# Attention's end and the routed feed-forward's start: scatters split, one normalisation moved to VectorE, unread matmuls, weights loaded later

## Chip, cores and metric

The kernel runs on one NeuronCore of one Trainium2 chip. The metric is the device time of one execution in microseconds (us); of several executions the median is taken.

## The reference, cut to what matters

The input x has two batches of 1024 rows of 256 values. Four pairs of layers follow one another, each `x = x + attention(layernorm(x))` and then `x = x + feed_forward(layernorm(x))`, with a context of 77 rows per batch. The change touches the last pair.

```
scores = einsum(Q, K) * scale + rel_pos_bias      # 16 heads, 77 keys
attn = softmax(where(mask, scores, -1e9))
x = x + (attn @ V, all heads) @ Wo
xf = layernorm(x)
eid = argmax(softmax(xf @ router_w + router_b))   # one of 8 experts
rank = number of earlier rows with the same expert
valid = rank < 320
y_e = relu(buf_e @ w1_e + b1_e) @ w2_e + b2_e     # rows that are valid
yov = relu(xf @ ow1 + ob1) @ ow2 + ob2            # rows over an expert's 320
x = x + where(valid, y_e, yov)
```

`ow1` and `ow2` are the overflow weights: they serve the rows that found their expert full.

## The kernel before, in words

x lives in SBUF as 16 tiles of 128 rows (`c.x`); the tiles of batch 0 are worked on first (`TOKEN_ORDER`), 8 of them (`HALF`), then those of batch 1. Each engine (SP for DMAs, POOL, DVE, ACT, PE) has its own program, and a step of one waits for semaphores that another raises.

**The last attention** (`attn_gqa`, L2046 to L2468) is a software pipeline over t = 0 to 15. In step t PE makes the scores of tile t (L2382). DVE adds the bias out of PSUM (L2195, L2197), takes the row maxima (L2200) and subtracts them (L2201); ACT takes the exponential (L2300); DVE sums it per head (L2211) and inverts the sums (L2212). POOL multiplies the probabilities by these inverses: that is the normalisation (L2108), 128x1232 values in place. Then PE transposes the probabilities (`prob_transpose`, L2396) in three groups, ACT copies them out of PSUM (L2307 to L2310), and PE multiplies them with the folded value weights (`output`, L2405, 10 products of two records each). DVE adds the result to x (L2206) and takes its statistics (L2265). POOL also adds the two halves of the rotary embedding of the next tile (L2105) ahead of each normalisation. The order on POOL's queue is that of its program: in step 14 (`t == NT - 2`) these are the rotary addition of tile 15, the normalisation of tile 14, and then the eight scatters of batch 0. In PE's program, the step after the last tile (`t == NT`, L2451) begins with 18 products whose results nobody reads (`keep_warm`, L107 to L110, bf16, 512 columns each), followed by the transposes of tile 15.

**Routing of batch 0** is woven into the same steps: router logits, expert and slot of each row are found while batch 1 is still in attention. `scatter_tile` (L1111, L1114) then writes one tile of 128 rows to its slots in the DRAM table `expert_rows`, by an indirect DMA out of POOL's queue, and raises `c.scat`. The slots come from L1083 (`r_slot_ok`).

**The last stage** (`moe3`, L2473 to L2840) is a block of its own, after the attention's block has ended on all engines and its semaphores are cleared (`free_semaphores`, L171 to L175). Its front: DVE finds the statistics (L200 to L215) and normalises the 8 tiles of batch 1 (L2609); PE transposes them (L2748) with ACT copying (L2712); PE makes the router logits (L1092, `pe_logits`) and turns them back (L1100); DVE finds experts and slots in a chain of some 25 small operations; POOL scatters the eight tiles of batch 1 (L1114). Meanwhile SP has loaded the small vectors, w1 and w2 of experts 0 and 1, and `ow1` (2 DMAs, L2545) and `ow2` (L2546). Then SP waits for all 16 scatters (`sp.wait_ge(c.scat, 16 * NT)`, L2547) and loads the rows of experts 0 to 3 and the overflow rows (L2534, L2540, L2553).

The body: for each of 8 experts DVE normalises the rows (L2640), PE transposes them (`x_transpose`, L2765), DVE copies (L2648 to L2651), PE makes the hidden layer (`hidden`, L2775, 32 records) with ACT's relu (L2722), and then the outputs (L2788, L2797), which DVE finishes and POOL writes to the output (L2580). w1 of expert e+2 is loaded by SP once `hidden(e)` is done (L2557, L2526). The overflow rows come last, in a loop (L2818 to L2840) that first waits for `ow_in` (L2816).

Of the kernel before, what the change touches and what calls it, by code (L numbers as in the profile page):

```python
# [6 lines left out]
P = 128  # L7
ALU = mybir.AluOpType
# [11 lines left out]
NT = T // P  # L20
# [5 lines left out]
HALF = NT // 2  # L26
PAD = 4
KC = D // P
SK = 77
# [25 lines left out]
def inside(i):  # L55

    return not is_static(i) or 0 <= i < NT
# [1988 lines left out]
def attn_gqa(c, d):  # L2046
# [48 lines left out]
    @programs.gpsimd  # L2095
    def _(pool):
        ng = nc.gpsimd

        def step(t, q):
            b = q % 2  # L2100
            if inside(t + 1) and t + 1 >= 1:
                i = t + 1
                pool.wait_ge(s["roped"], i + 1)
                wait(pool, s["qT_ps"], i * 2)
                ng.tensor_tensor(qr[:, :], t1[:, :], t2[:, :], ALU.add).then_inc(s["rope_ok"], 1)  # L2105
            if inside(t):
                pool.wait_ge(s["rd_ok"], t + 1)
                ng.tensor_tensor(heads(c.prob[b]), heads(c.prob[b]),  # L2108
                                 rden[b][:, :].unsqueeze(2).to_broadcast([P, HB, SK]), ALU.mult).then_inc(s["p_ok"], 1)
            if t == NT - 2:  # L2110
                pool.wait_ge(s["r_slot_ok"], 1)
                for k in range(HALF):
                    scatter_tile(c, r, k)
        for t in range(-1, NT):
            step(t, t % 4)

    @programs.vector
    def _(dve):
# [89 lines left out]
        def sums(t, b):  # L2208
            dve.wait_ge(s["exp_ok"], t + 1)
            wait(dve, s["p_ok"], t - 1)  # L2210
            links(nv.reduce_sum(c.den[:, :], heads(c.prob[b]), AX))  # L2211
            nv.reciprocal(rden[b][:, :], c.den[:, :]).then_inc(s["rd_ok"], 1)  # L2212

        layer_norm(1, 1)
        batch0 = slice(0, HALF)
# [129 lines left out]
    def _(pe):  # L2345
# [97 lines left out]
        def step(t, q):  # L2443
            b = q % 2
            banks_read(t)
            if inside(t):
                scores(t, b)
            if inside(t - 1):
                if t - 1 in (0, HALF):
                    pe.wait_ge(vw_in[t // HALF], 16 * 2)  # L2450
                if t == NT:  # L2451
                    keep_warm(c, c.ps[3], 18)
                prob_transpose(t - 1, 1 - b)
            if inside(t + 2):
                lnT(t + 2, b)
            if inside(t - 1):
                output(t - 1, 1 - b)
            if inside(t + 1):
                q_transpose(t + 1, 1 - b)
            route(t)  # L2460
            if inside(t + 2):
                queries(t + 2, b)
            back(t)
        step(-2, 2)
        keep_warm(c, c.ps[0], 12)
        for t in range(-1, NT + 1):
            step(t, t % 4)
    return programs  # L2468


# [2 lines left out]
def moe3(c, d):  # L2473
# [41 lines left out]
    with nc.Block() as block:  # L2515
        @block.sync
        def _(sp):
# [23 lines left out]
            for e in range(2):  # L2541
                load_w1(e)
                load_w2(e)
            for k in range(KC):
                sp.dma_start(ow1[:, k, :], d["L3_ffn_ow1"][k * P:(k + 1) * P, :]).then_inc(s["ow_in"], 16)  # L2545
            sp.dma_start(ow2[:, :, :], d["L3_ffn_ow2"].rearrange("(m p) n -> p m n", p=P)).then_inc(s["ow_in"], 16)  # L2546
            sp.wait_ge(c.scat, 16 * NT)  # L2547
            load_x(0)
            load_third(0)
            for e in range(1, 4):  # L2550
                load_x(e)
            load_third(1)
            sp.dma_start(Xo[:, :].rearrange("p (r n) -> p r n", n=XW),  # L2553
                         xd[OV0:OV0 + OVX * P, :].rearrange("(r p) n -> p r n", p=P)).then_inc(s["ox_in"], 16)
            for e in range(E3):
                if e + 2 < E3:
                    sp.wait_ge(s["h_ps"], e * MH + MH)  # L2557
                    load_w1(e + 2)
                if e % 2 == 1 and e + 2 < E3:
                    sp.wait_ge(s["y_ps"], third(e // 2) + 1)  # L2560
                    load_w2(e + 1)
                    load_w2(e + 2)
                if e >= 1 and e + 3 < E3:
                    for r in range(2):
                        written(sp, chunk(e - 1, r))
                    load_x(e + 3)
                if e % 2 == 0 and e >= 2 and e // 2 + 1 < E3 // 2:
                    written(sp, third(e // 2 - 1))
                    load_third(e // 2 + 1)
# [171 lines left out]
        def _(pe):  # L2741
            nt = nc.tensor

            def ln_transpose(n, k):
                pe.wait_ge(s["ln_ok"], n + 1)
                wait(pe, s["lnT_ok"], n - 2)
                for h in range(KC):
                    last = nt.transpose(c.ps[T3[n % 3]][:, h * P:(h + 1) * P], c.lnk[:, k * D + h * P:k * D + (h + 1) * P],  # L2748
                                        c.ident[:, :])
                last.then_inc(s["lnT_ps"], 1)  # L2750
            for n, k in enumerate(range(HALF, NT)):
                ln_transpose(n, k)
            pe.wait_ge(s["lnT_ok"], HALF)
# [47 lines left out]
            def over_transpose(n):  # L2801
                pe.wait_ge(s["oxl_ok"], n + 1)
                for k in range(KC):
                    last = nt.transpose(c.ps[0][:, k * P:(k + 1) * P], XLo[:, k * P:(k + 1) * P], c.ident[:, :])
                last.then_inc(s["oT_ps"], 1)
            x_transpose(0)
            for e in range(E3):
                hidden(e)
# [193 lines left out]
```

## Time and profile before

| what | value |
|---|---|
| median of 3 runs | 1050.93 us (1049.06 to 1051.18) |
| the profiled execution's own time | 1051.14 us |
| its span in the trace | 1049.3 us |
| PE busy | 910.5 us, 87% of the span |
| DVE busy | 714.4 us, 68% |
| POOL busy | 382.8 us, 36% |
| ACT busy | 377.4 us, 36% |
| mean granted TensorE clock | 0.95 of full |

The span is what the trace covers; the execution's own time is 1.84 us longer. A part by part account is made in the trace's time and then set against 1051.14. "PEclk" is the share of full TensorE clock that the chip granted: 1.00 is 2.4 GHz, 0.50 is 1.2 GHz, and a value between says that the clock changed inside the stretch. The page's line of 40 slices (26.2 us each) reads

```profile
PEclk9899989999989997988999999999999758999999
```

The two lowest digits, 7 and 5, stand in slices 32 and 33, from 813 to 866 us: the end of attention and the front of the last stage.

### The profile page before, as it was taken

Reading aid. Unit: us, or ns where it says so; the run is one execution under the profiler, and the core shown is the slowest. Engines: PE = TensorE matmul, PEld = TensorE weight load, DVE = VectorE, ACT = ScalarE, POOL = GpSimd, SP = SyncE. Lnnn points to the kernel's source line nnn. Section 1 sums busy time; section 2 is a strip of 40 time slices with the busy share of each in tenths; the row PEclk is TensorE's granted clock in tenths of the full one; section 3 lists DMA queues with packets and bytes.
Section 4 is the critical chain, followed back from the end, with each engine's and each line's share of the span. In section 5 each row is a group of like instructions: output and inputs, shape, how many; then the busy total and the mean of one; then the engine's idle time right before and its main releaser. Section 6 shows DMA issues by size and latency. Waiting matters only on the chain. (4 is left out here: it accounts for less than half of the span.)

```text
span 1049.3 us, 17056 instructions
## 1 busy us (share of the span) xinstructions
PE 910.5 (87%) x5799; PEld 648.5 (62%) x5803; DVE 714.4 (68%) x1579; ACT 377.4 (36%) x851; POOL 382.8 (36%) x282
## 2 busy tenths in 40 slices
PE   3899879999889985868899889999998619999997
PEld 2677744444567763743588467777766407777787
DVE  6788858888778877888377799999988222221211
ACT  2466541000155555753455143434333202213122
POOL 1566503423546642517355223333334220111111
PEclk9899989999989997988999999999999758999999
DMA  5000069999400007203465651111110294425300
GB/s 174 1 1 0 1 205 303 324 322 315 160 1 1 0 1 184 80 11 108 125 199 168 212 159 49 49 49 49 49 31 29 74 320 147 157 94 176 106 13 19
DMA packets 87256, 117.14 MB, mean 112 GB/s; under 512 B 12464, under 2 KB 75949, under 8 KB 86781
## 3 DMA queue, kind: packets, MB, share of 16 engines
q1 hardware_dynamic: 77455, 88.15, 27.7%
q10 hardware_dynamic: 4408, 15.46, 4.3%
q0 software_dynamic: 5328, 12.70, 3.4%
q8 instruction: 37, 0.61, 0.2%
q14 instruction: 28, 0.23, 0.1%
HBM read 68.08 MB, written 50.16 MB: 113 GB/s over the span
## 5 line engine op out<-in xcount | busy, mean ns | idle before, releaser
L925 PE MATMUL psum<-m_W,lnT 128*128 128x512 f32 x256 | 114.2, 598 | 0.8 <-DVE acc L837 0.8
L405 POOL TENSOR_TENSOR prob<-prob,a_rden 128x1232 f32<-128x1232 f32 x32 | 71.9, 2248 | 80.3 <-DVE a_rden L477 80.3
L925 PEld LDWEIGHTS psum<-m_W,lnT 128*128 128x128 f32 x256 | 47.2, 190 | 59.1 <-issue 56.7
L2722 ACT ACTIVATE prob<-psum,x_b 128x320 f32<-128x320 f32 x64 | 33.7, 527 | 127.5 <-PE psum L2775 127.5
L2405 PE MATMUL psum<-g_VW,pT 128*128 128x256 f32 (+1 forms) x320 | 75.3, 391 | 1.6 <-ACT pT L2310 1.6
L2775 PE MATMUL psum<-x_xT,x_w 128*128 128x320 f32 x256 | 72.7, 443 | 1.3 <-DVE x_xT L2649 1.3
L910 POOL TENSOR_TENSOR m_masked<-m_rel,m_mrow 128x1232 f32<-128x1232 f32 x16 | 41.8, 2616 | 79.8 <-DMA masked_bias<-m_masked 62.5
L2580 POOL DMA_INDIRECT out_x<-x_yt,x_X x20 | 19.8, 992 | 138.2 <-DVE x_yt L2663 138.2
L2405 PEld LDWEIGHTS psum<-g_VW,pT 128*128 128x128 f32 (+1 forms) x320 | 60.9, 194 | 13.3 <-ACT pT L2310 5.3
L2108 POOL TENSOR_TENSOR prob<-prob,g_rden 128x1232 f32<-128x1232 f32 x16 | 36.0, 2249 | 77.1 <-DVE g_rden L2212 77.1
L2775 PEld LDWEIGHTS psum<-x_xT,x_w 128*128 128x128 f32 x256 | 49.5, 195 | 23.0 <-issue 4.4
L2105 POOL TENSOR_TENSOR g_qr<-g_t 128x1024 f32<-128x1024 f32 x15 | 35.4, 2360 | 76.5 <-DVE g_t L2179 76.5
L2360 PE MATMUL psum<-g_Wq,lnT 128*128 128x512 f32 x128 | 59.6, 609 | 0.5 <-ACT lnT L2290 0.5
L2788 PE MATMUL psum<-x_w,prob 128*128 128x256 f32 x256 | 56.6, 379 | 0.0
L456 DVE TENSOR_REDUCE mx<-psum 128x16 f32<-128x1232 f32 x32 | 45.6, 1425 | 15.3 <-PE psum L595 15.1
L1275 POOL DMA_INDIRECT routed_results<-pT,m_idx x39 | 38.4, 984 | 38.8 <-issue 21.7
L2788 PEld LDWEIGHTS psum<-x_w,prob 128*128 128x128 f32 x256 | 48.0, 190 | 6.2
L396 POOL TENSOR_SCALAR ln<-x_tiles,mean,rstd 128x256 f32<-128x256 f32 x32 | 41.6, 1299 | 27.5 <-DVE rstd L426 25.6
L462 DVE TENSOR_TENSOR prob<-psum,mx 128x616 f32<-128x616 f32 x64 | 48.2, 794 | 3.0
L474 DVE TENSOR_REDUCE den<-prob 128x16 f32<-128x1232 f32 x32 | 45.7, 1427 | 4.4 <-ACT prob L517 4.1
L523 ACT ACTIVATE pT<-psum 128x512 f32<-128x512 f32 (+1 forms) x96 | 43.6, 527 | 13.7 <-PE psum L610 13.7
L2660 DVE TENSOR_TENSOR x_yt<-psum,x_b 128x256 f32<-128x256 f32 (+1 forms) x24 | 10.2, 424 | 52.3 <-PE psum L2788 41.3
(441 smaller groups left out, 2083.2 us busy)
## 6 DMA issues: line engine op xcount, KB each, us to landing
routed_rows<-hole SPq DMA_DIRECT2D x8, 2210.0 KB, 34.8
masked_bias<-m_masked ACTq DMA_DIRECT2D x16, 616.0 KB, 7.5
g_bias<-masked_bias SPq DMA_DIRECT2D x16, 616.0 KB, 3.8
x_w<-in_L_ffn_w SPq DMA_DIRECT2D x16, 512.0 KB, 4.6
x_w<-in_L_ffn_w SPq DMA_DIRECT2D x8, 1024.0 KB, 7.7
m_xb<-routed_rows SPq DMA_DIRECT2D x39, 130.0 KB, 2.1
m_rel<-in_rel_bias ACTq DMA_DIRECT2D x8, 616.0 KB, 9.8
expert_rows<-hole SPq DMA_DIRECT2D x1, 4680.0 KB, 35.3
```

The costliest lines, as they stand in the source:

```text
L396: nc.gpsimd.tensor_scalar(c.ln[b][:, :], xt(c, i), mean_of(c, i), rstd_of(c, i), ALU.subtract, ALU.mult).then_inc(ln_ok, 1)
L405: nc.gpsimd.tensor_tensor(heads(c.prob[b]), heads(c.prob[b]), rden[b][:, :].unsqueeze(2).to_broadcast([P, H, SK]), ALU.mult).then_inc(norm ...
L456: nv.reduce_max(c.mx[:, :].rearrange("p (r h) -> p r h", r=GROUPS), sview.rearrange("p r (h k) -> p r h k", k=SK), AX).then_inc(mx_ok, 1)
L462: nv.tensor_tensor(c.prob[b].rearrange("p (r h k) -> p r h k", r=GROUPS, k=SK)[:, r], sview[:, r].rearrange("p r (h k) -> p r h k", k=SK), ...
L474: nv.reduce_sum(c.den[:, :], heads(c.prob[b]), AX).then_inc(den_ok, 1)
L523: na.activation(c.pT[b][:, j0 * P:j1 * P], bank_pT[g][:, 0:(j1 - j0) * P], ACT.Copy).then_inc(pT_ok, 1)
L910: nc.gpsimd.tensor_tensor(masked[i % 2][:, :, :], rel[i // 2 % 2][:, :, :], mrow[:, i % 2, :].unsqueeze(1).to_broadcast([P, HB, SK]), ALU. ...
L925: last = nt.matmul(c.ps[p][:, :], c.lnT[b][:, k * P:(k + 1) * P], W[:, k, p * 512:(p + 1) * 512], start=(k == 0), stop=(k == KC - 1))
L2360: last = nt.matmul(c.ps[3 + u][:, :], c.lnT[b][:, k * P:(k + 1) * P], Wq[:, k, u * 512:(u + 1) * 512], start=(k == 0), stop=(k == KC - 1))
L2405: last = nt.matmul(bank_y[:, 0:D], c.pT[b][0:w, j * P:(j + 1) * P], VW[0:w, i // HALF, j, :], start=(j == 0), stop=(j == NB - 1))
L2775: last = nt.matmul(c.ps[2 + m % 4][:, 0:CAP], w1[b][:, k, m * P:(m + 1) * P], xT[b][:, k, :], start=(k == 0), stop=(k == KC - 1))
L2788: last = nt.matmul(c.ps[6 + ch % 2][:, 0:D], hT[b][:, m, r * P:(r + 1) * P], w2[b][:, m, :], start=(m == 0), stop=(m == MH - 1))
```

## The change

Six edits, all between the last two tiles of attention and the first expert:

1. POOL's step 14 issues the scatters of tiles 0 to 2 ahead of the normalisation of tile 14, and those of tiles 3 to 7 behind it.
2. The normalisation of tile 15 is done by DVE, right behind the inversion of its sums. POOL normalises tiles 0 to 14.
3. The 18 unread products ahead of the last `prob_transpose` become 8, and 6 are added behind the last `output`.
4. PE's program in the last stage begins with 10 unread products.
5. Behind the overflow transposes' definition, ahead of `x_transpose(0)`, PE waits for all 16 scatters and then issues 12 unread products.
6. SP loads `ow1` and `ow2` behind the rows of experts 0 to 3 and the overflow rows, instead of ahead of the wait for the scatters.

```diff
@@ attn_gqa, POOL @@
-            if inside(t):
+            if t == NT - 2:
+                pool.wait_ge(s["r_slot_ok"], 1)
+                for k in range(3):
+                    scatter_tile(c, r, k)
+            if inside(t) and t < NT - 1:
                 pool.wait_ge(s["rd_ok"], t + 1)
                 ng.tensor_tensor(heads(c.prob[b]), heads(c.prob[b]),
                                  rden[b][:, :].unsqueeze(2).to_broadcast([P, HB, SK]), ALU.mult).then_inc(s["p_ok"], 1)
             if t == NT - 2:
-                pool.wait_ge(s["r_slot_ok"], 1)
-                for k in range(HALF):
+                for k in range(3, HALF):
                     scatter_tile(c, r, k)
@@ attn_gqa, DVE, sums @@
             nv.reciprocal(rden[b][:, :], c.den[:, :]).then_inc(s["rd_ok"], 1)
+            if t == NT - 1:
+                dve.wait_ge(s["rd_ok"], t + 1)
+                nv.tensor_tensor(heads(c.prob[b]), heads(c.prob[b]), rden[b][:, :].unsqueeze(2).to_broadcast([P, HB, SK]),
+                                 ALU.mult).then_inc(s["p_ok"], 1)
@@ attn_gqa, PE @@
                 if t == NT:
-                    keep_warm(c, c.ps[3], 18)
+                    keep_warm(c, c.ps[3], 8)
                 prob_transpose(t - 1, 1 - b)
...
         for t in range(-1, NT + 1):
             step(t, t % 4)
+        keep_warm(c, c.ps[3], 6)
@@ moe3, SP @@
-            for k in range(KC):
-                sp.dma_start(ow1[:, k, :], d["L3_ffn_ow1"][k * P:(k + 1) * P, :]).then_inc(s["ow_in"], 16)
-            sp.dma_start(ow2[:, :, :], d["L3_ffn_ow2"].rearrange("(m p) n -> p m n", p=P)).then_inc(s["ow_in"], 16)
             sp.wait_ge(c.scat, 16 * NT)
...
                          xd[OV0:OV0 + OVX * P, :].rearrange("(r p) n -> p r n", p=P)).then_inc(s["ox_in"], 16)
+            for k in range(KC):
+                sp.dma_start(ow1[:, k, :], d["L3_ffn_ow1"][k * P:(k + 1) * P, :]).then_inc(s["ow_in"], 16)
+            sp.dma_start(ow2[:, :, :], d["L3_ffn_ow2"].rearrange("(m p) n -> p m n", p=P)).then_inc(s["ow_in"], 16)
@@ moe3, PE @@
+            keep_warm(c, c.ps[3], 10)
             for n, k in enumerate(range(HALF, NT)):
                 ln_transpose(n, k)
...
+            pe.wait_ge(c.scat, 16 * NT)
+            keep_warm(c, c.ps[3], 12)
             x_transpose(0)
```

## Rows read from the trace of the kernel before

**Rows 1.** Windows of 2 us: busy us (xcount) by engine, PEclk, DMA share, GB/s

```profile
820.00:822.00 2.00, 0.19 (x1) 0.19 (x2) 0.00 (x0) 0.00 (x0) 1.75 (x1) 0.97 0.19 67
...
834.00:836.00 2.00, 0.00 (x0) 0.00 (x0) 1.51 (x9) 1.37 (x2) 0.00 (x0) 0.88 0.11 19
...
872.00:874.00 2.00, 2.00 (x7) 1.31 (x6) 0.00 (x0) 0.53 (x1) 0.00 (x0) 0.73 0.68 221
```

**Rows 2.** The timeline, last but one tile of attention (start us, us, engine, line, what)

```profile
798.89 2.36 POOL L2105 TENSOR_TENSOR g_qr<-g_t 128x1024 f32<-128x1024 f32 x1 [5.47 <-DVE g_t L2179]
...
801.73 1.44 DVE L2201 TENSOR_TENSOR prob<-prob,mx 128x1232 f32<-128x1232 f32 x1
...
806.27 2.25 POOL L2108 TENSOR_TENSOR prob<-prob,g_rden 128x1232 f32<-128x1232 f32 x1 [5.02 <-DVE g_rden L2212]
...
808.58 1.09 PE L2396 MATMUL psum<-ident,prob 128*128 128x128 f32 x8 [0.75 <-POOL prob L2108]
...
810.87 1.44 DVE L2201 TENSOR_TENSOR prob<-prob,mx 128x1232 f32<-128x1232 f32 x1
...
810.95 4.59 PE L2405 MATMUL psum<-g_VW,pT 128*128 128x256 f32 x20 [0.53 <-ACT pT L2310]
...
811.26 1.89 POOL L1114 DMA_INDIRECT expert_rows<-x_tiles,acc  x1 [0.30 <-issue]
...
814.72 0.96 POOL L1114 DMA_INDIRECT expert_rows<-x_tiles,acc  x1 [0.30 <-issue]
...
815.08 0.25 DVE L2212 RECIPROCAL g_rden<-den 128x16 f32<-128x16 f32 x1
```

**Rows 3.** The timeline, last tile of attention and the end of that block

```profile
815.59 3.83 PE L110 MATMUL psum<-RQ,identb 128*128 128x512 bf16 x17
...
819.50 2.25 POOL L2108 TENSOR_TENSOR prob<-prob,g_rden 128x1232 f32<-128x1232 f32 x1
...
821.81 2.52 PE L2396 MATMUL psum<-ident,prob 128*128 128x128 f32 x10 [2.39 <-POOL prob L2108]
...
824.86 6.47 PE L2405 MATMUL psum<-g_VW,pT 128*128 128x256 f32 x20 [0.53 <-ACT pT L2310]
...
831.89 0.41 DVE L2265 BATCH_NORM_STATS2 bst<-x_tiles 128x6 f32<-128x256 f32 x1
```

**Rows 4.** The timeline, start of the last stage and its first TensorE work

```profile
833.87 1.28 ACT L220 ACT_TABLE_LOAD   x1 [9.06 <-PEq L175]
...
836.27 3.67 PE L2748 MATMUL psum<-ident,lnk 128*128 128x128 f32 x16 [4.95 <-DVE lnk L2609]
...
840.42 1.93 PE L1092 MATMUL psum<-lnT_all,qT 128*32 128x256 f32 x16 [0.47 <-ACT lnT_all L2712]
```

**Rows 5.** The timeline, the same logits products for batch 0, earlier

```profile
774.49 1.07 PE L1092 MATMUL psum<-lnT_all,qT 128*32 128x256 f32 x16
```

**Rows 6.** The timeline, from the first load of routed rows to expert 0

```profile
860.81 0.38 SPq L2534 DMA_DIRECT2D x_X<-expert_rows  x1
...
865.89 1.54 PE L2765 MATMUL psum<-ident,x_XL 128*128 128x128 f32 x6 [20.53 <-DVE x_XL L2640]
...
868.76 10.98 PE L2775 MATMUL psum<-x_xT,x_w 128*128 128x320 f32 x32 [1.33 <-DVE x_xT L2649]
```

**Rows 7.** Loads of routed rows between 859 and 868 us (tile view)

```profile
DMA to landing us min/median/max: 2.6/3.2/4.2
```

**Rows 8.** The timeline, the same two steps of expert 1 and 2, later

```profile
886.93 8.78 PE L2775 MATMUL psum<-x_xT,x_w 128*128 128x320 f32 x32
...
895.54 0.82 PE L2765 MATMUL psum<-ident,x_XL 128*128 128x128 f32 x6
```

**Rows 9.** The timeline of SP's queue, and TensorE at expert 2

```profile
842.07 4.80 SPq L2545 DMA_DIRECT2D x_ow<-in_L_ffn_ow  x2
...
879.78 16.77 SPq L2526 DMA_DIRECT2D x_w<-in_L_ffn_w  x4
...
906.80 8.88 PE L2775 MATMUL psum<-x_xT,x_w 128*128 128x320 f32 x32
```

## Prediction

> **What bounds the kernel now.** I read the page's clock line first, then the windows, then the timeline between 795 and 907 us. TensorE is busy nearly everywhere, so time can only be won where it waits or runs at half clock. All six edits lie in the one stretch where it does both.
>
> In the last attention, each tile goes from the inverse sums through the normalisation to the transposes and the output. For tile 14 this is tight: normalisation at 806.27, transposes at 808.58, output ending at 810.95 + 4.59 = 815.54, all at full clock [rows 2]. For tile 15 the inverse is ready at 815.33 [rows 2], but POOL starts its normalisation at 819.50, since eight scatters stand ahead of it; the transposes begin at 821.81, after a pause of 2.39 us [rows 3]. The clock fell from 2.4 to 1.2 GHz inside 820 to 822, after TensorE had done 0.19 us of work in those 2 us [rows 1]. Transposes and output then took 821.81 to 824.86 + 6.47 = 831.33, that is 9.52 us, where tile 14 took 815.54 - 808.58 = 6.96.
>
> The last stage begins at 833.87 [rows 4], 1.57 us after DVE's last work of the old block (832.30) [rows 3]. The clock fell again between 834 and 836, with no TensorE work there [rows 1], so the first transposes and the logits products ran at half clock [rows 4]; the same products took 1.07 us for batch 0 [rows 5] and 1.93 here. After that come DVE's chain and POOL's eight scatters, which no edit touches. Then rows are loaded from 860.81, and the first `x_transpose` and most of `hidden(0)` run at half clock until inside 872 to 874 [rows 1, 6].
>
> **Part by part.**
>
> Edits 1 and 2, the normalisations. The new start of tile 15's transposes is the later of two. DVE: the inverse ends at 815.33; the multiplication has the shape and the two SBUF inputs of L2201, 1.44 us [rows 2], so it is done at 816.82. TensorE: its unread products start at 815.59, 18 of them in 3.83 us (17 are recorded), 0.213 each [rows 3]; 8 take 1.70, until 817.30. The later one is 817.30. The gain is 821.81 - 817.30 = **4.51**. What is late next is thus TensorE itself, with 0.48 us in hand against DVE. Queued behind DVE's multiplication is the residual of tile 14, some 1.5 us later than now; output 15 waits for it, but only 2.37 us after its transposes start, so it is hidden by 2 us.
>
> POOL's queue: the rotary addition ends at 801.25, the slots come from step 13, so three scatters go from about 801.4 on, and the normalisation of tile 14 is wanted at 806.27 [rows 2]. A scatter costs 0.96 and 0.30 between two [rows 2], so three end near 805.2. One scatter of eight took 1.89: it was issued at 811.26, inside an L2201 that ran from 810.87 to 812.31 [rows 2], and ended 0.84 after it. The second of the three falls inside the L2201 at 801.73; stretched likewise it ends at 804.0 and the third at 805.3. Normalisation 14 keeps its start: cost **0**. Bounds: a gain is excluded, since 806.27 is set by DVE's inverse; if all three took 1.89 with 0.30 between, the third would end at 801.4 + 6.3 = 807.7, costing 1.4. I take 0, the bound next to the one collision the trace shows.
>
> Whether the first scatter, under way when L2201 starts, would hold up DVE no row shows well. The Trainium skill (SBUF — State Buffer, "SBUF: two separate sides") says that a DVE instruction with two SBUF inputs and a GpSimd instruction that reads SBUF lock each other out, whichever started first holding the shared ports to its end. The stretched scatter agrees with that.
>
> Edit 3, clock. With no pause ahead of tile 15, transposes and output should take tile 14's 6.96 us instead of 9.52: gain **2.56** (bounds 0 and 2.56), end at 824.26. The 6 products behind the output take 1.28, to 825.54; DVE's tail of 832.30 - 831.33 = 0.97 would end at 825.23. The block now ends with TensorE, 0.31 later: cost **0.31** (0 if the barrier hides it).
>
> Edit 4. Ten products at full clock take 2.13 us, from 833.87 to 836.00 in old time, and the first transposes start at 836.27 when DVE has a tile ready [rows 4]: hidden, by 0.27. Only 1.6 us without TensorE work now lie before them, instead of 831.33 to 836.27, so I expect full clock. Logits: 1.93 - 1.07 = **0.86** [rows 4, 5]. Transposes: 16 in 3.67, two a tile, 0.46; ACT copies tile by tile behind them and will set the pace, so I count half of one tile, **0.25** (bounds 0 and 1.8, half of 3.67).
>
> Edit 5. The wait asks for what the row loads wait for anyway, and only `x_transpose(0)` is queued behind it. Twelve products start at about 860.81; all at half clock they take 12 x 0.426 = 5.11, until 865.92, against transposes at 865.89 [rows 6]: cost 0.03 at most, and nothing once the clock rises. At full clock the six transposes take 0.82 instead of 1.54, gain **0.72**, and `hidden` 8.78 to 8.88 instead of 10.98, gain **2.15** [rows 6, 8, 9]. The rise in the kernel before came after some 4.3 us of steady products (868.76 to about 873) [rows 1, 6], and the twelve last about that long. Bounds: 0 and 2.87.
>
> Edit 6. SP's three issues move behind the row loads; the two of `ow1` took 4.80 us of SP's time [rows 9]. The next that SP has to do is w1 of expert 2 at 879.78, used at 906.80: 27 us in hand [rows 9]. The overflow step is 140 us away. In their old place they kept the DMA queues busy until shortly before the row loads. These landed in 2.6 to 4.2 us [rows 7]; at best all come at 2.6, a gain of up to 1.6. I take **0**.
>
> Sum: 4.51 + 2.56 - 0.31 + 0.86 + 0.25 + 0.72 + 2.15 = **10.74** gained. The profiled execution's own time is 1051.14, which gives 1040.4; that execution lies 0.21 above the median of 1050.93, inside the spread of the runs. About 0.2% (2.1 us) is what a measurement of this kernel can tell from no change.
>
> **Rivals.**
>
> A. The warm-up ahead of the experts misses: the clock rises late, or falls again in the 1.3 us in which DVE copies between transposes and `hidden(0)`. For it: twelve products last barely as long as the rise took before. The 2.87 is lost: 1043.3. Chance 0.12.
>
> B. The clock is at half when the last stage starts. The ten products take 4.26, until 838.13, the transposes start 1.86 late, and 0.86 + 0.25 is lost: 1043.4. Against it: the six products in front are meant to bridge, and the pause is shorter than the 2.39 us before the fall at 820 to 822. Chance 0.08.
>
> C. Tile 15 still runs at half clock: 2.56 lost, 1043.0. Against it: no pause of over 1 us is left there. Chance 0.05.
>
> D. The first scatter holds DVE's ports: L2201 at 801.73 waits until the scatter ends near 802.4, 0.7 us, and the inverse, normalisation 14 and all behind it move along: 1041.1. For it: two SBUF inputs against a descriptor write. Against it: the scatter before the stretched one was still running when the L2201 of 810.87 started, and that one kept its 1.44 [rows 2]. By the Trainium skill's section just named, the first to start holds the ports for its whole instruction; the trace shows no DVE instruction held up. Chance 0.08.
>
> E. Slower. The late overflow weights push w1 of expert 2 out. The place is SP's queue and the DMA queues between the overflow rows and L2526, and it decides once w1 lands after 906.80 in old time: the 27 us must be used up first. To end slower by 2.1 it would have to use them up and add 13 more, as with 15 more: 1055.4. Nothing in the trace lasts like that; SP's longest two issues are 4.80. Chance 0.02.
>
> F. The edits do not do what they say: tile 15 starts early, but a wait further on, such as the block's end or the row loads, takes the gain back, within 2.1 of before: 1050. The timeline shows no second chain that long. Chance 0.02.
>
> **The numbers.** My forecast, 1040.4, has 0.63, and by the small bounds lies between 1038.8 (row loads 1.6 shorter) and 1041.8 (normalisation 14 late by 1.4). The range 1038.8 to 1043.5 takes in A, B, C and D; two of the clock rivals together would leave it. All of these are faster: 0.96. Same is F, 0.02; slower is E, 0.02.
>
> **What would show it.** Right: three scatters between 801 and 806; normalisation 14 at 806.3; transposes of tile 15 at 817.3 with a granted clock of 1.00 to the end of output; the last stage 6.8 us earlier, its logits products near 1.07 us; `x_transpose(0)` 7.9 us earlier than 865.89, at 0.82 us; `hidden(0)` near 8.8 us; nothing changed behind it. Wrong: a clock of 0.50 in any of these, a pause of TensorE at expert 2, a DVE step 14 that is late, or a gain in a stretch that I left alone.

## The result and the profile after

The changed kernel took 1041.24 us in the median of 5 runs (1039.85 to 1043.00), the kernel before 1049.06 in the median of 5 on the same chip (1047.06 to 1051.18). The ratio is 0.9926, 95% interval 0.9904 to 0.9948: faster by 0.5 to 1.0%. The profiled execution took 1039.85 us, 11.3 less than the profiled one of before; the medians differ by 7.8. Why these two differ is taken up below. The ratios in this document leave out executions that lie more than 1.5% above the fastest of the same kernel.

The page's first line, and its clock line in slices of 26 us, after the change:

```profile
span 1038.1 us, 17090 instructions
...
PEclk9899989999989997987999999999999969999999
```

The dip of 7 and 5 in slices 32 and 33 has become 9 and 6. The timeline of the same execution (start us, us, engine, line, what), from step 14 of attention to expert 0:

```profile
800.96 1.01 POOL L1114 DMA_INDIRECT expert_rows<-x_tiles,acc  x1 [0.15 <-issue]
...
801.28 1.44 DVE L2204 TENSOR_TENSOR prob<-prob,mx 128x1232 f32<-128x1232 f32 x1
...
802.27 1.29 POOL L1114 DMA_INDIRECT expert_rows<-x_tiles,acc  x1 [0.30 <-issue]
...
803.87 0.96 POOL L1114 DMA_INDIRECT expert_rows<-x_tiles,acc  x1 [0.30 <-issue]
...
805.01 3.29 PE L2389 MATMUL psum<-g_KB,g_qT 128*128 128x154 f32 x16 [2.50 <-ACT g_qT L2303]
...
805.83 2.24 POOL L2112 TENSOR_TENSOR prob<-prob,g_rden 128x1232 f32<-128x1232 f32 x1 [1.01 <-DVE g_rden L2215]
...
808.13 2.31 PE L2403 MATMUL psum<-ident,prob 128*128 128x128 f32 x10
...
812.07 1.55 POOL L1114 DMA_INDIRECT expert_rows<-x_tiles,acc  x1 [0.30 <-issue]
...
815.55 0.25 DVE L2215 RECIPROCAL g_rden<-den 128x16 f32<-128x16 f32 x1
...
815.62 1.67 PE L110 MATMUL psum<-RQ,identb 128*128 128x512 bf16 x7
...
815.84 1.44 DVE L2218 TENSOR_TENSOR prob<-prob,g_rden 128x1232 f32<-128x1232 f32 x1
...
817.34 1.09 PE L2403 MATMUL psum<-ident,prob 128*128 128x128 f32 x8
...
819.71 4.59 PE L2412 MATMUL psum<-g_VW,pT 128*128 128x256 f32 x20 [0.53 <-ACT pT L2317]
...
827.14 1.28 ACT L220 ACT_TABLE_LOAD   x1 [7.49 <-PEq L175]
...
829.55 2.71 PE L2756 MATMUL psum<-ident,lnk 128*128 128x128 f32 x16
...
832.74 1.07 PE L1092 MATMUL psum<-lnT_all,qT 128*32 128x256 f32 x16 [0.47 <-ACT lnT_all L2720]
...
849.78 0.96 POOL L1114 DMA_INDIRECT expert_rows<-x_tiles,acc  x1 [0.30 <-issue]
...
852.24 0.38 SPq L2542 DMA_DIRECT2D x_X<-expert_rows  x1
...
852.27 4.45 PE L110 MATMUL psum<-RQ,identb 128*128 128x512 bf16 x10 [15.45 <-DMA expert_rows<-x_tiles,acc]
...
857.36 0.88 PE L2774 MATMUL psum<-ident,x_XL 128*128 128x128 f32 x6
...
859.58 8.85 PE L2784 MATMUL psum<-x_xT,x_w 128*128 128x320 f32 x32 [1.33 <-DVE x_xT L2657]
```

Three scatters now lie ahead of the normalisation of tile 14, which starts at 805.83 (before: 806.27 [rows 2]). Tile 15 is normalised by DVE at 815.84, its transposes start at 817.34 (before: 821.81 [rows 3]), and its output takes 4.59 instead of 6.47. The last stage starts at 827.14 (before: 833.87 [rows 4]), its first transposes take 2.71 instead of 3.67, its logits products 1.07 instead of 1.93, and the hidden layer of expert 0 takes 8.85 instead of 10.98 [rows 4, 6].

The windows of 2 us (busy us and instructions of PE, PEld, DVE, ACT, POOL; PEclk; DMA share; GB/s):

```profile
806.00:808.00 2.00, 2.00 (x11) 1.92 (x9) 0.51 (x3) 0.00 (x0) 2.00 (x1) 0.57 0.00 0
...
822.00:824.00 2.00, 2.00 (x11) 1.77 (x10) 0.00 (x0) 0.00 (x0) 0.00 (x0) 1.00 0.00 0
...
858.00:860.00 2.00, 0.67 (x5) 0.38 (x4) 1.72 (x6) 0.00 (x0) 0.00 (x0) 1.00 0.93 286
```

The clock is full through tile 15's output and through the copies ahead of the hidden layer. It was at half for a while between 806 and 810, where the profiled execution of before was at full. That slowed tile 15's scores, which PE makes in this stretch, and tile 14's transposes (2.31 us for all ten, where before they ran from 808.58 to 810.42, 1.84 us). The scores of before:

```profile
805.46 2.36 PE L2382 MATMUL psum<-g_KB,g_qT 128*128 128x154 f32 x16 [2.48 <-ACT g_qT L2296]
```

In the thirteen other profiles of this document, the kernels that keep POOL's old order among them, the same scores took 3.22 to 4.03 us. So the change didn't bring this half clock: the one execution without it is the one that the prediction read.

To compare executions, I cut each into the same pieces, from starts and ends in the timeline. Each piece ends where the next begins: A, start of tile 14's normalisation to tile 15's transposes; B, to the end of tile 15's output; C, to the start of the last stage; D, to the end of its logits products; E, to the first load of rows; F, to DVE's first work on them; G, to the hidden layer of expert 0; H, to the transposes of expert 1. "Rest" is all behind that, "start" the time at which A begins.

| kernel (profiled execution) | start | A | B | C | D | E | F | G | H | A to H | rest |
|---|---|---|---|---|---|---|---|---|---|---|---|
| before | 806.27 | 15.54 | 9.52 | 2.54 | 8.48 | 18.46 | 3.96 | 3.99 | 10.83 | 73.32 | 169.71 |
| change | 805.83 | 11.51 | 6.96 | 2.84 | 6.67 | 18.43 | 3.93 | 3.41 | 8.69 | 62.44 | 169.83 |
| change, again | 804.95 | 11.98 | 6.96 | 2.84 | 6.67 | 18.49 | 4.04 | 3.33 | 10.38 | 64.69 | 169.76 |
| change, third | 810.68 | 11.49 | 6.95 | 2.85 | 6.67 | 18.44 | 3.64 | 3.72 | 8.68 | 62.44 | 169.78 |
| moves alone | 810.40 | 13.57 | 6.89 | 2.55 | 8.27 | 18.42 | 4.03 | 4.00 | 10.63 | 68.36 | 169.74 |
| unread alone | 808.73 | 14.68 | 9.99 | 2.85 | 6.66 | 19.85 | 3.83 | 3.32 | 8.69 | 69.87 | 169.80 |
| late weights alone | 805.61 | 15.20 | 8.59 | 2.54 | 8.43 | 18.47 | 4.21 | 3.99 | 10.60 | 72.03 | 169.76 |
| change, weights early | 806.00 | 12.11 | 6.96 | 2.84 | 6.66 | 19.77 | 3.87 | 3.32 | 8.69 | 64.22 | 169.78 |
| change, no twelve | 807.36 | 11.80 | 6.96 | 2.85 | 6.66 | 18.77 | 3.96 | 4.00 | 10.26 | 65.26 | 169.78 |
| change, no six and ten | 807.53 | 11.44 | 6.96 | 2.53 | 7.77 | 18.45 | 3.87 | 3.33 | 8.69 | 63.04 | 169.83 |
| change, POOL normalises | 810.09 | 13.12 | 6.96 | 2.85 | 6.67 | 18.47 | 3.42 | 3.33 | 8.69 | 63.51 | 169.80 |
| products throughout | 809.57 | 11.97 | 6.95 | 2.85 | 6.66 | 18.45 | 4.96 | 3.33 | 8.69 | 63.86 | 169.77 |
| the same, again | 809.86 | 11.55 | 6.95 | 2.85 | 6.67 | 18.46 | 4.45 | 3.32 | 8.69 | 62.94 | 169.80 |
| change, four between | 812.24 | 11.88 | 6.96 | 2.85 | 6.66 | 18.44 | 3.72 | 3.32 | 8.69 | 62.52 | 169.84 |

Two things stand out. The rest is 169.7 to 169.8 in all fourteen: nothing behind expert 0's hidden layer changed. And the start of A lies anywhere between 805.0 and 812.2, with no order by kernel. Of the edits only the three scatters lie ahead of it, and they don't set it: it follows the start of DVE's inverse by 0.33 or 0.34 us in all fourteen. The chip may have a part in it, since the four executions on one chip start at 805.0 to 810.4 and the three on another at 809.9 to 812.2.

The ratios below can't rank the changed kernel and its variants: all their intervals overlap. What an edit is worth is therefore read from the pieces, of one execution per variant.

### The profile page after: what moved, and what is told of

Its sections match the earlier page's. It is cut to its first block and busy times, and to the rows that moved or that the text cites. A ratio compares the mean times of both kernels' runs of the same rounds, so it can differ in the third digit from the quotient of the medians.

```text
span 1038.1 us, 17090 instructions
## 1 busy us (share of the span) xinstructions
PE 912.5 (88%) x5815; PEld 648.8 (63%) x5821; DVE 713.1 (69%) x1580; ACT 377.0 (36%) x851; POOL 382.1 (37%) x281
## 5 line engine op out<-in xcount | busy, mean ns | idle before, releaser
L2784 PE MATMUL psum<-x_xT,x_w 128*128 128x320 f32 x256 | 70.6, 434 | 1.3 <-DVE x_xT L2657 1.3
L2112 POOL TENSOR_TENSOR prob<-prob,g_rden 128x1232 f32<-128x1232 f32 x15 | 33.7, 2249 | 73.1 <-DVE g_rden L2215 73.1
L840 DVE SCALAR_TENSOR_TENSOR acc<-psum,gates,acc 128x256 f32<-128x256 f32 x96 | 40.3, 477 | 9.6 <-PE psum L925 9.5
```

What stands on the lines that cost most here:

```text
L2784: last = nt.matmul(c.ps[2 + m % 4][:, 0:CAP], w1[b][:, k, m * P:(m + 1) * P], xT[b][:, k, :], start=(k == 0), stop=(k == KC - 1))
```

## The experiments

**The change again, twice.** No edit. First:

> The changed kernel once more, beside the kernel before on the same chip. The two profiled executions differed by 11.3 us, the medians of five runs by 7.8. Theory: the profiled execution of before was one with more half clock than most (the clock falls at slightly different moments in each execution), so the typical gain is the 7 to 9 us of the medians. Rival: the medians were off by drift between chips, and the gain is the 10.7 us of the prediction. Theory: ratio near 0.9920; rival: near 0.9898.

Measured: ratio 0.9938 (0.9912 to 0.9964), over 34 runs of before that lay between 1044.54 and 1056.22. The interval holds the theory's 0.9920 and leaves out the rival's 0.9898. But the theory's reason covers only a part: the profile shows that the changed kernel, too, can lose time inside the stretch. TensorE's timeline of that execution:

```profile
857.05 0.88 PE L2774 MATMUL psum<-ident,x_XL 128*128 128x128 f32 x6 [0.31 <-DVE x_XL L2648]
...
859.26 10.54 PE L2784 MATMUL psum<-x_xT,x_w 128*128 128x320 f32 x32 [1.33 <-DVE x_xT L2657]
```

and its windows (columns as above):

```profile
856.00:858.00 2.00, 1.61 (x9) 0.74 (x7) 1.03 (x4) 0.00 (x0) 0.00 (x0) 0.97 0.95 303
858.00:860.00 2.00, 0.74 (x2) 0.63 (x3) 1.76 (x6) 0.00 (x0) 0.00 (x0) 0.88 0.88 276
860.00:862.00 2.00, 2.00 (x5) 1.22 (x5) 0.00 (x0) 0.43 (x1) 0.00 (x0) 0.50 1.07 370
```

The six transposes ran at full clock, and then the clock fell inside 858 to 860, in the pause of 1.33 us in which DVE copies. The hidden layer took 10.54 us. This is rival A of the prediction. Of the seven profiled executions that have the twelve products and nothing between transposes and hidden layer, it is the only one (H of 10.38; 8.68 or 8.69 in the other six).

The third:

> The changed kernel a third time. Theory: its stretch from tile 14's normalisation to the end of expert 0's hidden layer is 62.4 us where the clock holds into the hidden layer and 64.7 where it falls, and all the rest of the spread between executions (several us) arises ahead of that normalisation, which started between 805.0 and 810.4 us in the profiles so far. Rival: the stretch itself varies by over 3 us.

Measured: ratio 0.9894 (0.9861 to 0.9927). Its stretch A to H is 62.44, the same as the first one's, though A starts 4.85 later. The stretches of the three executions differ by 2.25 at most, so the rival's 3 us was not seen. Of the 2.25, 1.69 lie in H, by the clock ahead of expert 0, as the theory said; 0.47 more lie in A, which the theory left out. The interval of the ratio holds both the 0.9920 and the 0.9898 of the first expectation, so the question of the typical gain is open again; it is taken up below. One small cost shows here: the rows landed early (F of 3.64), the twelve products were still running, and G is 3.72 instead of 3.3 to 3.4.

**The moves alone** (edits 1 and 2 on the kernel before):

```diff
+            if t == NT - 2:
+                pool.wait_ge(s["r_slot_ok"], 1)
+                for k in range(3):
+                    scatter_tile(c, r, k)
-            if inside(t):
+            if inside(t) and t < NT - 1:
...
+            if t == NT - 1:
+                dve.wait_ge(s["rd_ok"], t + 1)
+                nv.tensor_tensor(heads(c.prob[b]), heads(c.prob[b]), rden[b][:, :].unsqueeze(2).to_broadcast([P, HB, SK]),
+                                 ALU.mult).then_inc(s["p_ok"], 1)
```

> The kernel before with the two moves of edits 1 and 2 alone (three scatters ahead of normalisation 14, tile 15 normalised by DVE); unread products and weight loads as before. Theory of the prediction: the transposes of tile 15 now start where the 18 unread products end, 3.83 us behind 815.6, so 2.4 us are won, and with the pause gone its 2.56 us of half clock: 4.9 us in all, ratio 0.9953. Rival, the clock alone matters and the moves win nothing by themselves: ratio 1.000. Second rival, the moves carry the whole change: ratio 0.992 or lower.

Measured: ratio 0.9971 (0.9952 to 0.9991), stretch 68.36, that is 4.96 less than before. TensorE's timeline:

```profile
826.28 4.58 PE L2412 MATMUL psum<-g_VW,pT 128*128 128x256 f32 x20 [0.53 <-ACT pT L2317]
...
835.82 3.67 PE L2755 MATMUL psum<-ident,lnk 128*128 128x128 f32 x16 [4.95 <-DVE lnk L2616]
```

The output is back at 4.58 us with no new product at all: once the pause is gone the clock holds. The front is untouched, 3.67 as before. The ratio's interval holds the theory's 0.9953 at the edge and excludes both rivals. That the stretch came so close to 4.9 is partly luck: A gave 1.97 where the theory had 2.4, B gave 2.63 where it had 2.56, and 0.41 came from D and H, which these edits don't touch.

**The unread products alone** (edits 3, 4 and 5 on the kernel before):

```diff
-                    keep_warm(c, c.ps[3], 18)
+                    keep_warm(c, c.ps[3], 8)
...
+        keep_warm(c, c.ps[3], 6)
...
+            keep_warm(c, c.ps[3], 10)
...
+            pe.wait_ge(c.scat, 16 * NT)
+            keep_warm(c, c.ps[3], 12)
```

> The kernel before with edits 3, 4 and 5 alone (unread products 8 instead of 18, and 6, 10 and 12 new ones). Theory: the front gains 1.1 us and expert 0 up to 2.9 us of full clock, less 0.3 for the block's end; tile 15 still waits for POOL: 3.7 us, ratio 0.9965. Rival: with only 8 products ahead of a pause of 4.5 us the clock falls earlier there and the gain is 2 us or less, ratio 0.998 or above.

Measured: ratio 0.9974 (0.9950 to 0.9997), stretch 69.87, 3.45 less than before. The interval holds both expectations; the pieces tell more. D and H came down as the theory said (6.66 and 8.69), B went up a little (9.99), as the rival said, and E went up by 1.4, which nobody had said. A is 0.86 shorter for no reason of these edits: POOL's eight scatters took 9.95 us in this execution and 10.80 in that of before, where one was stretched to 1.89. The timeline, with tile 15's output, the last scatter and the first load behind it:

```profile
825.83 7.57 PE L2405 MATMUL psum<-g_VW,pT 128*128 128x256 f32 x20 [0.53 <-ACT pT L2310]
...
858.93 0.96 POOL L1114 DMA_INDIRECT expert_rows<-x_tiles,acc  x1 [0.30 <-issue]
...
862.76 0.38 SPq L2535 DMA_DIRECT2D x_X<-expert_rows  x1
```

and the windows there:

```profile
858.00:860.00 2.00, 0.00 (x0) 0.00 (x0) 0.00 (x0) 0.00 (x0) 1.59 (x2) 0.50 1.07 398
...
860.00:862.00 2.00, 0.00 (x0) 0.00 (x0) 0.00 (x0) 0.00 (x0) 0.00 (x0) 0.50 0.90 341
```

The last scatter needs 3.83 us from its issue to the load that waits for it, where the changed kernel needs 852.24 - 849.78 = 2.46, and the DMA share is still 0.90 in 860 to 862. (In the changed kernel it was 0.18 to 0.37 between 846 and 852.)

**The late weights alone** (edit 6 on the kernel before: the three loads of `ow1` and `ow2` behind that of the overflow rows).

> The kernel before with edit 6 alone (overflow weights loaded behind the row loads). Theory: nothing, ratio 1.000 within 0.001. Rival: with the DMA queues free the row loads land up to 1.6 us earlier, ratio 0.9985.

Measured: ratio 1.000 (0.9979 to 1.0021). E and F are 18.47 and 4.21, against 18.46 and 3.96: no load came earlier. The theory holds. What its stretch has less than before (1.29) lies in A and B, ahead of the edit, in pieces at half clock. Since this edit does nothing there, its profile is a second sample of the kernel before: 73.3 and 72.0.

**The change with the weights early** (edit 6 alone undone), run because of the 19.85 above:

```diff
+            for k in range(KC):
+                sp.dma_start(ow1[:, k, :], d["L3_ffn_ow1"][k * P:(k + 1) * P, :]).then_inc(s["ow_in"], 16)
+            sp.dma_start(ow2[:, :, :], d["L3_ffn_ow2"].rearrange("(m p) n -> p m n", p=P)).then_inc(s["ow_in"], 16)
             sp.wait_ge(c.scat, 16 * NT)
```

> The changed kernel with edit 6 undone: the overflow weights loaded ahead of the wait for the scatters again. In the run with the unread products alone, which has the weights early, the time from the end of the logits products to the first load of rows was 19.85 us, against 18.4 to 18.8 in all other profiles, because the last scatter landed 3.83 us after its issue instead of 2.4. Theory: the faster front moves the last scatter into the time in which the overflow weights still fill the DMA queues, so edit 6 is worth 1.4 us with edits 3 and 4 and nothing without them: here 19.8 us, and the stretch 63.8 instead of 62.4. Rival: that was chance, here 18.5 and 62.4.

Measured: E is 19.77; ratio to the kernel before 0.9932 (0.9909 to 0.9955). Last scatter and first load:

```profile
850.53 0.96 POOL L1114 DMA_INDIRECT expert_rows<-x_tiles,acc  x1 [0.30 <-issue]
...
854.34 0.38 SPq L2542 DMA_DIRECT2D x_X<-expert_rows  x1
```

3.81 us between them, as with the unread products alone. The stretch is 64.22, of which 0.6 is a longer half clock in A (12.11 against 11.51); without it 63.6. The theory stands, twice seen: edit 6 is worth 1.3 to 1.4 us, but only together with the faster front. In the kernel before, the last scatter was issued 858.37 - 833.87 = 24.5 us after the stage's start and was complete 2.44 us later, at 860.81; in these two kernels it was issued 22.6 to 22.7 us after the start. The times from issue to landing of the stage's eight scatters (tile view of `expert_rows`, POOL alone) show the cause more directly:

| kernel | shortest | median | longest |
|---|---|---|---|
| before | 2.4 | 5.1 | 5.9 |
| change, weights early | 3.8 | 5.5 | 6.0 |
| change | 2.4 | 2.7 | 4.9 |

With the overflow weights in flight at least half of the scatters take over 5 us, in the kernel before too. There the last of the weight loads, issued at 846.91, landed 11.9 us later, at 858.8, 0.4 us behind the issue of the last scatter, which then needed only 2.4; and the last one to land decides when the row loads start. Here that load was issued at 841.01 and landed 12.5 us later, at 853.5, 3 us behind the issue of the last scatter.

**The change without the twelve** (edit 5 undone):

```diff
-            pe.wait_ge(c.scat, 16 * NT)
-            keep_warm(c, c.ps[3], 12)
             x_transpose(0)
```

> The changed kernel without edit 5 (no wait and no 12 unread products ahead of the first transposes of the experts). From the start of tile 14's normalisation to the end of expert 0's hidden layer the profiled changed kernel took 62.4 us in one execution and 64.7 in another, in which the clock fell again ahead of the hidden layer. Theory: without the twelve, transposes and most of the hidden layer run at half clock always: 65.3 us. Rival: the twelve win nothing on average, because the clock rises and falls anyway: under 64 us here too.

Measured: ratio to before 0.9939 (0.9910 to 0.9968), stretch 65.26, the theory's 65.3. TensorE:

```profile
859.48 1.54 PE L2774 MATMUL psum<-ident,x_XL 128*128 128x128 f32 x6 [20.77 <-DVE x_XL L2648]
...
862.36 10.42 PE L2784 MATMUL psum<-x_xT,x_w 128*128 128x320 f32 x32 [1.34 <-DVE x_xT L2657]
```

Against 0.88 and 8.85 in the changed kernel. The agreement of the sum is partly luck (A and E are 0.3 longer here than in the changed kernel, for no reason of this edit). The other three executions without the twelve (before, moves alone, late weights alone) are like this one: G of 3.99 or 4.00, H of 10.60 to 10.83. By G and H together, 14.26 here and 14.59 to 14.82 in those three, the twelve win 1.9 to 2.8 us where the clock holds (12.01 to 12.40) and 0.55 to 1.1 where it falls (13.71).

**The change without the six and the ten** (the second half of edit 3 and edit 4 undone):

```diff
-        keep_warm(c, c.ps[3], 6)
...
-            keep_warm(c, c.ps[3], 10)
```

> The changed kernel without the 6 unread products behind the last output and without the 10 at the start of the last stage. Theory: the block ends 0.3 us earlier, and the front (start of the last stage to the end of its logits products, 6.7 us in the changed kernel) is back at half clock and takes 8.5. Rival: the pause is now short enough by itself, since tile 15 ends at full clock, and the front stays at 6.7 to 7.2.

Measured: ratio to before 0.9917 (0.9888 to 0.9945). C is 2.53 instead of 2.84, the 0.3 as expected. D is 7.77, between the 8.5 of the theory and the 7.2 of the rival:

```profile
830.88 3.67 PE L2755 MATMUL psum<-ident,lnk 128*128 128x128 f32 x16 [4.95 <-DVE lnk L2616]
...
835.02 1.21 PE L1092 MATMUL psum<-lnT_all,qT 128*32 128x256 f32 x16 [0.47 <-ACT lnT_all L2719]
```

The transposes ran at half clock as in the kernel before (3.67), and the clock rose just ahead of the logits products (1.21). The sixteen products thus win 1.10 in D and give back 0.31 in C: 0.8 us in this execution, up to 1.5 where the clock rises later, as in the kernel before. What the six and the ten win each by themselves was not tried.

**The change with POOL normalising tile 15** (edit 2 undone, the scatters split):

```diff
-            if inside(t) and t < NT - 1:
+            if inside(t):
...
-            if t == NT - 1:
-                dve.wait_ge(s["rd_ok"], t + 1)
-                nv.tensor_tensor(heads(c.prob[b]), heads(c.prob[b]), rden[b][:, :].unsqueeze(2).to_broadcast([P, HB, SK]),
-                                 ALU.mult).then_inc(s["p_ok"], 1)
```

> The changed kernel with tile 15 normalised by POOL again, its scatters still split. Theory: POOL's last scatter ends 0.9 us before the inverse is ready, so the normalisation starts 5 ns to 0.1 us behind it and takes 2.25 instead of 1.44: the transposes of tile 15 start 0.8 us later, nothing else changes. Rival: moving the work to DVE is what wins the 4.5 us, and without it the transposes start 3 us later or more.

Measured: ratio to before 0.9914 (0.9882 to 0.9947), stretch 63.51. Inverse, normalisation and transposes:

```profile
820.57 0.25 DVE L2215 RECIPROCAL g_rden<-den 128x16 f32<-128x16 f32 x1
...
820.91 2.24 POOL L2112 TENSOR_TENSOR prob<-prob,g_rden 128x1232 f32<-128x1232 f32 x1 [2.27 <-DVE g_rden L2215]
...
823.21 0.86 PEld L2399 LDWEIGHTS psum<-ident,prob 128*128 128x128 f32 x8 [1.94 <-POOL prob L2112]
```

From the start of the inverse to the transposes it is 2.64 us, in the changed kernel 817.34 - 815.55 = 1.79: 0.85 more, as the theory had it, and far from the rival's 3 us. The split of the scatters is what wins; the move to DVE adds 0.85 to it. (The other 0.76 by which A is longer here lies ahead of the inverse: tile 15's scores took 4.00 us, against 3.29.)

**Products through the whole pause.** Since the clock can fall ahead of expert 0, TensorE was kept at unread products from the moment the slots are known:

```diff
+            pe.wait_ge(s["slot_ok"], 1)
+            keep_warm(c, c.ps[3], 40)
             pe.wait_ge(c.scat, 16 * NT)
-            keep_warm(c, c.ps[3], 12)
+            keep_warm(c, c.ps[3], 18)
             x_transpose(0)
+            keep_warm(c, c.ps[3], 4)
```

> The changed kernel with unread products through the whole pause ahead of the experts: 40 once the slots are known, 18 instead of 12 once all scatters have landed, and 4 between the first transposes and the first hidden layer. Theory: the clock is full by the time the rows arrive and stays so, in every execution; the hidden layer takes 8.8 us, the stretch from tile 14's normalisation to its end 62.3 us, and the median is 1 us below the changed kernel's. Rival: the clock falls at the copies all the same, or the products delay the transposes by over 0.5 us, and nothing is won.

> The kernel with unread products through the whole pause, again, beside the changed kernel on one chip. In its first profile the clock held, but the first routed rows arrived 4.96 us after the issue of their load, against 3.4 to 4.2 in all other profiles. Theory: chance; this time 4.2 or less, the stretch at 62.5 us, and a median 1 us below the changed kernel's. Rival: the many products delay the loads (their instructions have to be fetched too): again 4.7 or more, and no gain over the changed kernel.

Measured: ratios to before 0.9901 (0.9861 to 0.9940) and 0.9916 (0.9884 to 0.9948); the changed kernel beside the second had 0.9894 (0.9861 to 0.9927). The clock held both times, H is 8.69. But the first rows came late both times, 4.96 and 4.45 us after the issue of their load:

```profile
844.79 10.29 PE L110 MATMUL psum<-RQ,identb 128*128 128x512 bf16 x40 [3.89 <-DVE acc L1083]
...
856.34 0.38 SPq L2542 DMA_DIRECT2D x_X<-expert_rows  x1
...
860.79 1.06 DVE L2648 TENSOR_SCALAR x_XL<-x_X 128x256 f32<-128x256 f32 x3 [14.82 <-DMA x_X<-expert_rows]
```

The second theory asked for 4.2 or less and its rival for 4.7 or more; 4.45 is neither. In the other twelve profiles the piece is 3.4 to 4.2, so these two lie above all of them. The traces bear out the rival's reason in part. In the 1 us from 857.34 of the second (and likewise from 857.45 of the first) the DMA view has one packet of 0.02 MB on the queue that it calls "instruction" (q8), and no other profile has one from 8 us ahead of the first row load to 9 us behind it. In both, one of SP's issues of row loads took longer than usual: 1.32 and 0.91 us, against 0.59 at most in the changed kernel. So it looks as if the products cost what they bring, but that this packet, and not something else, held up the load is not shown. No gain over the changed kernel was measured.

**Four products between** the first transposes and the hidden layer, the twelve kept:

```diff
             x_transpose(0)
+            keep_warm(c, c.ps[3], 4)
```

> The changed kernel with 4 unread products between the first transposes and the first hidden layer, the 12 ahead of them kept. Theory: the pause of 1.3 us in which the clock fell in one execution is filled with 0.9 us of work, so the hidden layer takes 8.8 to 9.3 us in every execution, and the stretch 62.4 us. Rival: the clock has not always risen by then, and the hidden layer still takes over 9.5 us in some.

Measured: ratio to before 0.9917 (0.9888 to 0.9946), stretch 62.52, the hidden layer at full clock:

```profile
863.86 0.87 PE L2774 MATMUL psum<-ident,x_XL 128*128 128x128 f32 x6
...
864.57 1.03 PE L110 MATMUL psum<-RQ,identb 128*128 128x512 bf16 x4
...
866.07 8.85 PE L2784 MATMUL psum<-x_xT,x_w 128*128 128x320 f32 x32 [0.47 <-DVE x_xT L2657]
```

The pause shrinks from 1.33 to 0.47 us at no cost (H and G as in the best executions). But this is one profile, and without the four the clock held in six of seven. That the four prevent the fall is not shown; the timing, with a spread of several microseconds between executions, can't tell 0.7 us.

## Why the prediction was right, and where not

The predicted 1040.4 lies 0.8 from the median, and the range held it. That it lies so near is partly luck: the forecast started from 1051.14, 2.1 above the median of before measured beside the change (1049.06), and took off 10.7, where the medians differ by 7.8. Term by term, in the profiled pair:

| term | predicted | measured |
|---|---|---|
| earlier transposes of tile 15 | 4.51 | 4.03 |
| tile 15 at full clock | 2.56 | 2.56 |
| block ends with TensorE | -0.31 | -0.30 |
| logits products, transposes of the front | 0.86 + 0.25 | 1.81 |
| transposes and hidden layer of expert 0 | 0.72 + 2.15 | 2.72 |
| late weights | 0 | 0.06 |
| sum | 10.74 | 10.88 |

The start of A came 0.44 earlier and the rest took 0.12 longer, which makes the 11.2 of the spans. The sums agree better than their terms, since what the first term has too much the fourth has too little.

**Edits 1 and 2.** The mechanism was as told: with POOL's scatters out of the way, tile 15's transposes start when DVE and TensorE are done. One step of it was wrong: "What is late next is thus TensorE itself, with 0.48 us in hand against DVE". Here both were ready at 817.3, and in five of the nine executions in which DVE normalises tile 15 behind eight products, the transposes waited for DVE, as in the second one of the changed kernel:

```profile
816.93 1.09 PE L2403 MATMUL psum<-ident,prob 128*128 128x128 f32 x8 [0.30 <-DVE prob L2218]
```

The reason is the half clock at tile 15's scores, on which DVE's chain waits: they took 0.86 to 1.52 us longer than in the execution that the prediction was read from. A is 11.44 to 12.11 in these nine, where the prediction's numbers make it 817.30 - 806.27 = 11.03, so the term was 0.4 to 1.1 too large, 0.48 in this pair. Rival F falls.

**The scatters and DVE.** Right for the reason given, and rival D is excluded by a row: the L2204 at 801.28 started 0.32 into a scatter and kept its 1.44 us. The scatters issued inside such an instruction were stretched, to 1.29 and 1.55, and each ended 0.83 or 0.84 after it, like the one of before. The same holds for 25 scatters over all fourteen profiles (0.83 to 0.85). The Trainium skill (SBUF — State Buffer, "SBUF: two separate sides") has whoever starts first hold the ports to the end of its instruction; here the traces agree where DVE was first, in those 25 cases, but not where the scatter was: then DVE kept its 1.44 or 1.45 us.

**Edit 3, clock.** Right, and rival C never came: 6.95 or 6.96 in all ten executions with split scatters and eight products. The moves alone gave 6.89, so the pause was the whole cause, not the number of products. Right to the hundredth is luck: in the second sample of before (late weights alone) B was 8.59, and 1.6 would have been won. Nor must every pause go: where POOL normalises, one of 1.45 us was left ahead of tile 15, and the clock held.

**Edit 4.** The mis-sized term: "half of one tile, 0.25" for the front's transposes. They took 3.67 before and 2.71 after, 0.96 less. I had ACT's copies set the pace behind them; the half-rate transposes did, and at full clock they keep up with DVE's eight normalisations (2.68). Rival B never came: D is 6.66 or 6.67 in all ten executions with the ten products.

**Edit 5.** The sizes were right (0.88 and 8.85 us). Rival A, put at 0.12, came in one of seven executions. The cost of "0.03 at most" was too low (0.07 in the profiled pair): with rows that land early, the twelve delayed the transposes by 0.4 in the third execution.

**Edit 6.** "I take 0" was read from the kernel before, and it failed as a statement on the edit. In that kernel it is 0, as its run alone shows, but the front that edits 3 and 4 speed up would have run into the weights' transfer. In the changed kernel the edit is worth 1.3 to 1.4 us, as a cost avoided. The sum came out right since it was reckoned from a before in which this cost did not yet exist. Rival E is excluded: the rest is unchanged.

**Why 11.3 in the profiled pair and 7.8 in the medians.** The spread between executions is larger than I had taken it for. In one set the kernel before lay between 1044.54 and 1056.22, and "about 0.2% is what a measurement can tell" was too fine for it: the intervals here are 0.4 to 0.8% wide. The profiles show where the spread arises: A starts between 805.0 and 812.2. Inside the stretch the kernel before has 73.3 and 72.0, the changed one 62.4, 62.4 and 64.7; their means differ by 9.5. The three measured ratios are 0.9926, 0.9938 and 0.9894 (the medians differ by 7.8, 8.2 and 10.2 us). Weighted by their intervals, they give 0.9923, give or take 0.0015: a gain of 8 us, between 6.5 and 9.6. So 10.7 fits an execution in which the clock holds, beside one of before that lost much, and is 1 to 4 us too much for the typical one. Why the start of A wanders stays open. Half clock ahead of it does not explain it by itself: up to 800 us, by windows of 5 us, the clock was at half for 61.4 us in the execution that started at 806.27 and for 61.3 in one that started at 810.09.

## What to carry to other kernels

Look for work without a deadline that stands ahead of a step on the critical path in an in-order queue: splitting it around that step, with a faster engine for the step itself and fewer unread products ahead of the next, won 4.0 us in the profiled pair and, by ending the pause, another 2.6 of clock. A margin of tenths of a microsecond between two engines should be looked up in a second profile: the one that the forecast was read from was the only one of fourteen in which the scores ran at full clock. When a stage gets faster, ask which transfer it now runs into, since a load that was harmless where it stood can start to cost. And before an edit is sized to a microsecond, compare several executions piece by piece: one pair of profiles said 11.3 us where three sets of runs together give 8, between 6.5 and 9.6.

## What the runs showed of the hardware

- A scatter issued by POOL inside a DVE `tensor_tensor` with both inputs in SBUF was held until 0.83 to 0.85 us after that instruction's end, in 25 cases. One issued up to 0.9 us ahead of it was not held up, and DVE took 0.01 us longer at most. Once the two started within 0.02 us of each other: then the scatter kept its 0.96 us, and DVE took 1.49 instead of 1.44.
- The clock fell from 2.4 to 1.2 GHz not only after long pauses: once it did so in a pause of 1.33 us that followed some 0.9 us of transposes and a pause of 0.3, and six times it held through a like sequence.
- It also fell with TensorE at work again: after the pauses of 2.39, 2.99 and 1.59 us ahead of tile 15 (before, unread alone, late weights alone) it fell about 0.1, 1.7 and 2.3 us behind the start of the transposes, by an estimate from the mean clock of the 2 us windows.
- An indirect scatter that is complete 2.4 us after its issue when the DMA engines are nearly idle needs 3.8 to 6.0 while weight loads (2 MB of them issued ahead of it) are under way.
- The same tile of attention, behind identical code but for three scatters that don't delay it, was reached up to 7 us apart in fourteen executions on several chips.
